# Channel attention: part of the softmax denominator through accumulating DMAs, a one-column border from PSUM, and chain openings on ScalarE

## The chip, the cores and the metric

The kernel runs as one program on one NeuronCore of a Trainium2 chip. The time is device microseconds from launch to end, the median of several executions. Engines are named as in the profile: PE is TensorE (matmuls and transposes), PEld its weight loads, DVE is VectorE, ACT is ScalarE, POOL is GpSimd, SP is SyncE.

## What is computed

Four residual layers on `x` of shape 4 x 256 x 64 x 64, each behind a group normalisation. The change lies in the third, the channel attention. Cut to what matters:

```python
half = cout // 2
x_pad = jnp.pad(x, ((0, 0), (0, 0), (PAD, PAD), (PAD, PAD)))      # PAD = 3, K = 7
q    = jnp.einsum('bchw,oc->bohw', x, w_q)
kmap = jnp.einsum('bchw,oc->bohw', x_pad, w_k)
vmap = jnp.einsum('bchw,oc->bohw', x_pad, w_v)
kwin, vwin = _unfold2d(kmap, K), _unfold2d(vmap, K)               # 7 x 7 windows
kwin = jnp.concatenate([kwin[:, :half] + rel_h, kwin[:, half:] + rel_w], axis=1)
attn = jax.nn.softmax(q[..., None] * kwin.reshape(b, cout, h, w, K * K), axis=-1)
out  = jnp.sum(attn * vwin.reshape(b, cout, h, w, K * K), axis=-1)
x    = x + out
```

Every channel and pixel has its own softmax over the 49 taps of its window.

## The kernel before, in words

**Tiling.** `channel_attention` handles 16 bands of 16 image rows (4 images x 4). A band has 256 channels, two halves of 128 partitions, and each half is cut into two tiles of 8 rows, 512 pixels. So a band is four tiles, t = 0 to 3, and the layer is 64 tiles. A tile has 49 taps; tap j is written (o, i) = divmod(j, 7), and I call the seven taps of one o a row of taps.

**One tap, four engines.** DVE (`multiply`, L1991) writes (key window + bias) x query into one of three PSUM banks `stage`. PE (`shift`, L1677) subtracts an upper bound `top` from it by a matmul with minus the identity. ACT (`exponential`, L1845) writes the exponential into `se`, a ring of four rows of taps. POOL (`weigh`, L1892) multiplies by the value window, four taps and then three of a row in one instruction, into `ev`. PE adds up both: `sum_exponential` adds the exponential of tap j-2 into the bank `pe_sum`, `sum_weighted` adds the product of tap j-12 into `pv_sum`. Both use `add_up` (L1684): four 128 x 128 transposing matmuls that accumulate in PSUM.

**What orders the work.** There is no scheduler: each engine's queue is written out in tap order and waits on semaphores. PE's step j is: `sum_weighted` of j-12, `shift` of j, `sum_exponential` of j-2. `multiply` of tap j waits for the exponential of tap j-3, which frees its bank, so DVE is at most three taps ahead. `exponential` waits, at the first tap of a group, until the slot's old values have been added up and weighed.

**Extra work in the steps.** While half H is worked on, the next half is prepared. PE projects keys, queries and values into `pj` (`project`, L1666, at the steps of `PROJ_AT`: K1, K2, Q1, Q2 when t is even, V1 and V2 when t is odd; each has two matmuls, which the trace shows as two instructions each). ACT copies them out. DVE builds `near`, the largest and the smallest key of each row or column of seven, in two levels: `near_step_of` first takes pairs into `pair` (L1938, from `pj` and the keys), then reduces (L1946). For the half whose windows run along columns of the image (H even, built in t = 2) a border of 3 columns at both sides of `pair` is first filled by a `tensor_scalar` from the zero columns of the keys (L1931, four times per band). Then 34 links (`extreme_step`, at the steps `EXT_AT`, in even tiles from step 34 on and in odd tiles) turn `near` into the bound `top`: four chains of 7 additions and maxima (or minima), whose opening link is a `tensor_scalar` (L1965) and whose others are L1967, then products and maxima (L1974, L1976). DVE also inverts the denominator of the tile before (`invert`, L1999, steps 3, 5, 7, 9; `take_e_sums`, L1833, copies it out of PSUM at step 1), divides (L2007, step 12) and adds the residual (step 23).

The few lines that set PE's order in a tap:

```python
if not late and (t * NTAP + j >= V_LAG or not first):
    sum_weighted(n, *before(t, j, V_LAG), first=first)
shift(n, t, j)
if t * NTAP + j >= E_LAG or not first:
    sum_exponential(n, *before(t, j, E_LAG), first=first)
```

## Time and profile before

| | us |
|---|---|
| median of 3 runs | 8098.6 |
| lowest, highest | 8085.5, 8104.4 |
| span of the profiled execution | 8087.0 |
| of it, channel attention's 64 tiles | from about 3310 to 7405 |

The profiled execution itself is one of those whose span is 8087.0 us from the first to the last instruction; what lies around the span is 11.6 us against the median. Over the span PE is busy 93%, DVE 72%, POOL 56%, ACT 45%. Within channel attention (3600 to 7100 us) PE is busy 96%, DVE 91%, POOL 80% and ACT 50%.

The rows are read like this. A busy time is a share of an engine's own time; instructions of PE and DVE overlap a little with their successors, so what one of them costs in a dense stretch is the distance from its start to the next one's start, which the timeline shows. A bracket behind a row is the engine's idle time just before it and what ended it.

### The profile page before, as it was taken

To read this page: it belongs to the slowest core of one execution; us is meant where nothing else is said; L and a number is where in the kernel's file an instruction comes from. 1 tells how busy PE (TensorE), PEld (TensorE's weight loads), DVE (VectorE), ACT (ScalarE), POOL (GpSimd) and SP (SyncE) were. 2 spreads that over 40 slices of the span, in tenths; PEclk is the share of its full clock that TensorE was granted. 3 is DMA by queue.
4 is the path that set the end of the run, shared out by engine and by line. 5 is a ranking of instruction groups with operands and counts; after the bars stand their busy time and mean duration, and the time that the engine had idled before them with its cause. 6 is when DMAs were issued, how large, how long until landed. Compare 5 with 4: busy or idle time off the path is not lost. (4 is left out here: it accounts for less than half of the span.)

```text
span 8087.0 us, 141762 instructions
## 1 busy us (share of the span) xinstructions
PE 7551.7 (93%) x55106; PEld 6507.3 (80%) x55106; DVE 5845.1 (72%) x8981; ACT 3601.8 (45%) x6912; POOL 4566.7 (56%) x2002
## 2 busy tenths in 40 slices
PE   5999998999997998799999999999999999997999
PEld 4777776789997775588888888888888888886899
DVE  5666665334442555798998999999999989996664
ACT  3556554333332332345445454545545454554222
POOL 3555552033331001588777887878878787886232
PEclk9999998999998999899999999999999999998999
DMA  3111114855557772100000000000000000002452
GB/s 144 57 60 66 56 62 137 277 152 146 148 146 215 220 206 85 25 19 19 24 21 21 18 18 26 18 20 19 20 27 18 15 21 24 23 12 79 144 163 81
DMA packets 633017, 617.20 MB, mean 76 GB/s; under 512 B 465525, under 2 KB 498421, under 8 KB 627174
## 3 DMA queue, kind: packets, MB, share of 16 engines
q1 hardware_dynamic: 581318, 483.44, 21.5%
q0 software_dynamic: 33856, 96.69, 3.3%
q10 hardware_dynamic: 17376, 30.54, 1.0%
q8 instruction: 330, 5.41, 0.3%
q14 instruction: 137, 1.12, 0.0%
HBM read 397.01 MB, written 193.76 MB: 73 GB/s over the span
## 5 line engine op out<-in xcount | busy, mean ns | idle before, releaser
L1892 POOL TENSOR_TENSOR e_ev<-e_se,e_v 128x2048 f32<-128x2048 f32 (+1 forms) x896 | 3307.9, 3712 | 858.9 <-ACT e_se L1845 856.5
L1845 ACT ACTIVATE e_se<-e_stage 128x512 f32<-128x512 f32 x3136 | 1868.5, 598 | 2038.3 <-PE e_stage L1677 1991.5
L1991 DVE SCALAR_TENSOR_TENSOR e_stage<-e_k,e_rl,e_qp 128x512 f32<-128x512 f32 x3136 | 2299.7, 746 | 250.1 <-ACT e_se L1845 199.3
L1684 PE MATMUL e_pe_sum<-e_ident,e_se 128*128 128x128 f32 x12544 | 1888.5, 273 | 16.4 <-ACT e_se L1845 12.2
L1684 PE MATMUL e_pv_sum<-e_ident,e_ev 128*128 128x128 f32 x12544 | 1881.1, 273 | 0.5 <-POOL e_ev L1892 0.5
L1684 PEld LDWEIGHTS e_pe_sum<-e_ident,e_se 128*128 128x128 f32 x12544 | 1556.7, 140 | 261.3 <-ACT e_es L1833 21.8
L1677 PE MATMUL e_stage<-e_top,e_minus 128*128 128x512 f32 x3136 | 1513.4, 483 | 163.1 <-DVE e_stage L1991 160.9
L1684 PEld LDWEIGHTS e_pv_sum<-e_ident,e_ev 128*128 128x128 f32 x12544 | 1483.0, 141 | 205.7 <-issue 203.7
L911 POOL DMA_DIRECT2D agg<-c_ot x384 | 334.6, 874 | 880.6 <-ACT c_ot L989 771.0
L403 POOL TENSOR_TENSOR a_pr<-a_pr,a_rden 128x480 f32<-128x480 f32 x512 | 494.6, 987 | 547.2 <-DVE a_rden L636 547.2
L1677 PEld LDWEIGHTS e_stage<-e_top,e_minus 128*128 128x128 f32 x3136 | 598.2, 191 | 219.6 <-DVE e_stage L1991 185.2
L596 ACT ACTIVATE a_pr<-a_ps,a_nmax 128x240 f32<-128x240 f32 x1024 | 459.2, 460 | 386.1 <-DVE a_nmax L630 386.1
L1967 DVE SCALAR_TENSOR_TENSOR e_ext<-e_near,e_rl,e_ext 128x512 f32<-128x512 f32 x768 | 574.9, 749 | 0.9
L948 PE MATMUL c_pa<-c_x_high,c_w_high 128*128 128x448 f32 (+1 forms) x1440 | 523.0, 363 | 33.2 <-DVE c_w_low L1014 33.2
L630 DVE TENSOR_REDUCE a_nmax<-a_ps 128x2 f32<-128x480 f32 x512 | 312.8, 652 | 292.4 <-PE a_ps L484 285.2
L948 PE MATMUL c_pa<-c_x_low,c_w_high 128*128 128x448 f32 (+1 forms) x1440 | 522.7, 363 | 0.0
L948 PE MATMUL c_pa<-c_x_high,c_w_low 128*128 128x448 f32 (+1 forms) x1440 | 522.5, 363 | 0.0
L2287 PE MATMUL f_pc<-f_x_high,f_w_high 128*128 128x256 f32 x1536 | 440.4, 287 | 14.0 <-DVE f_xr L2467 11.8
L1946 DVE TENSOR_REDUCE e_near<-e_pair 128x192 f32<-128x768 f32 (+1 forms) x392 | 436.1, 1113 | 0.5
L2287 PE MATMUL f_pc<-f_x_low,f_w_high 128*128 128x256 f32 x1536 | 434.8, 283 | 0.0
L2287 PE MATMUL f_pc<-f_x_high,f_w_low 128*128 128x256 f32 x1536 | 434.2, 283 | 0.0
L2244 POOL TENSOR_TENSOR f_x_low<-f_xt,f_x_high 128x2560 fp32r<-128x2560 f32 x32 | 186.2, 5819 | 438.3 <-ACT f_x_high L2321 406.6
(175 smaller groups left out, 11663.9 us busy)
## 6 DMA issues: line engine op xcount, KB each, us to landing
qkv<-b_ot SPq DMA_DIRECT2D x120, 512.0 KB, 5.9
c_xt<-qkv SPq DMA_DIRECT2D x384, 160.0 KB, 3.8
agg<-c_ot POOLq DMA_DIRECT2D x384, 160.0 KB, 2.5
f_ws<-in_L_w_sets SPq DMA_DIRECT2D x32, 1152.0 KB, 8.0
a_xb<-in_x SPq DMA_DIRECT2D x24, 768.0 KB, 5.1
a_xr<-in_x SPq DMA_DIRECT2D x32, 512.0 KB, 3.8
x<-a_xr SPq DMA_DIRECT2D x32, 512.0 KB, 2.7
b_xc<-x SPq DMA_DIRECT2D x32, 512.0 KB, 6.0
```

What stands on the lines that cost most here:

```text
L403: nc.gpsimd.tensor_tensor(w, w, by, ALU.mult).then_inc(normalised, 1)
L596: last = nc.scalar.activation(pr[P % BUF][:, i, e, :], ps[:, 2 * s + i, e * NK:(e + 1) * NK], ACT.Exp, bias=nmax[P % BUF][:, i, e:e + 1], ...
L911: pool.dma_start(dst, ot[u][:, b]).then_inc(stored[u], 16)
L948: last = nc.tensor.matmul(pa[:, u, r, 0:(last_ - first) * WW].rearrange("p (k c) -> p k c", c=WW), lhsT=w[u][:, dx].rearrange("p o y -> p ...
L1677: nc.tensor.matmul(stage[:, bank_of(t, j), :], lhsT=minus[:], rhs=top[h][:, u * TPX:(u + 1) * TPX], start=False, stop=True, skip_group_che ...
L1684: last = nc.tensor.matmul(acc[:, c * PART:(c + 1) * PART], lhsT=src[:, c * PART:(c + 1) * PART], rhs=ident[:], is_transpose=True, start=j ...
L1845: nc.scalar.activation(se[(t * K2 + o) % NSE][:, i], stage[:, bank_of(t, j), :], ACT.Exp)\
L1892: nc.gpsimd.tensor_tensor(split(ev[(t * NG2 + g) % NEV][:, 0:size]), split(se[(t * K2 + o) % NSE][:, i:i + size]), window(v[h], h, u, o, i ...
L1946: nc.vector.tensor_reduce(grid(near[:, i])[:, first + low:first + low + part, PAD:PAD + WW], pairs, AX.XY, op)\
L1967: nc.vector.scalar_tensor_tensor(rows(ext[:]), win, r[:, o:o + 1], rows(ext[:]), ALU.add, op)\
L1991: nc.vector.scalar_tensor_tensor(rows(stage[:, bank_of(t, j), :]), win, rl[:, h, o:o + 1], rows(qp[:]), ALU.add, ALU.mult).then_inc(multip ...
L2287: last = nc.tensor.matmul(pc[:, m, s], lhsT=w[:, m, s * KW3 + dy, h], rhs=x[u][:, s, h, rows], start=dy == 0 and h == 0 and i == 0, stop=d ...
```

## The change

Three edits, all in channel attention.

1. **Exponentials partly added by DMA.** The exponentials of the first four taps of row 0 go into a new buffer `acc` instead of `se` (two buffers, by tile parity). For rows 1 to 4 of taps (`GATHERED`), after POOL has weighed the row, POOL issues a DMA that adds the row's first four exponentials (128 x 2048 numbers, 1 MiB) onto `acc`. Each such DMA waits until the one before has landed. PE no longer adds these 20 taps one by one. It adds the four columns of `acc` at steps 44 to 47, and before the first it waits until all four DMAs of the tile have landed. So PE makes 33 sums of exponentials per tile instead of 49.
2. **Border.** The `tensor_scalar` over 3 columns at both sides becomes a `tensor_tensor` over one column at the left, from the zero column of the keys and the first projected column in PSUM; the wait behind it is dropped.
3. **Opening links.** The four opening links of the chains are made by ACT (an Identity activation with bias) instead of DVE; `EXT_AT` is spread anew, with three places instead of one between an opening link and the next.

```diff
+        acc = [sb(f"acc{u}", [PART, ROW_PARTS[0][1], TPX]) for u in range(2)]
...
+        GATHERED = (1, 2, 3, 4)
+        NACC = ROW_PARTS[0][1]
+        DIRECT = [j for j in range(NTAP) if j % K2 >= NACC or j // K2 not in (0, *GATHERED)]
+        NES = len(DIRECT) + NACC
+        ACC_AT = (44, 45, 46, 47)
...
-        EXT_AT = [EXT_FREE[s * len(EXT_FREE) // NEXT_] for s in range(NEXT_)]
+        OPENS = [0, CHAIN[0], 2 * CHAIN[0], 2 * CHAIN[0] + CHAIN[1]]
+        LINK_AT = [sum(3 if i - 1 in OPENS else 1 for i in range(1, s + 1)) for s in range(NEXT_ + 1)]
+        EXT_AT = [EXT_FREE[LINK_AT[s] * len(EXT_FREE) // LINK_AT[-1]] for s in range(NEXT_)]
...
+            def sum_gathered(n, t, i):
+
+                if i == 0:
+                    pe.wait_ge(gathered, gathers(n, t, K2))
+                add_up(pe_sum, acc[t % 2][:, i], False, False).then_inc(e_summed, 1)
...
-                if t * NTAP + j >= E_LAG or not first:
+                if (t * NTAP + j >= E_LAG or not first) and before(t, j, E_LAG)[1] in DIRECT:
                     sum_exponential(n, *before(t, j, E_LAG), first=first)
+                if j in ACC_AT:
+                    sum_gathered(n, t, ACC_AT.index(j))
...
+            def open_extreme(H, s):
+
+                act.wait_ge(near_step, nears(H + 1))
+                act.wait_ge(ext_step, exts(H, s))
...
+                nc.scalar.activation(rows(ext[:]), win, ACT.Identity, bias=rl[:, h, 0:1]).then_inc(ext_step, 1)
...
+            def gather(n, t, o):
+
+                if o == GATHERED[0]:
+                    pool.wait_ge(weighted, tiles(n, t, NG2, 1))
+                else:
+                    pool.wait_ge(gathered, gathers(n, t, o - 1))
+                flat = lambda x: x.rearrange("p i n -> p (i n)")
+                pool.dma_start(flat(acc[t % 2][:]), flat(se[(t * K2 + o) % NSE][:, 0:NACC]), accum_op=ALU.add).then_inc(gathered, 16)
...
                         weigh(n, t, g, first=n == 0)
+                        if g % 2 and g // 2 in GATHERED:
+                            gather(n, t, g // 2)
...
-                        edge = [[PW, size], [WW + 2, 2], [1, PAD]]
-                        nc.vector.tensor_scalar(bass.AP(tensor=a.tensor, offset=a.offset, ap=[a.ap[0]] + edge),
-                                                bass.AP(tensor=z.tensor, offset=z.offset, ap=[z.ap[0]] + edge), 0.0, None, op)\
-                            .then_inc(near_step, 1)
-                        dve.wait_ge(near_step, nears(H) + near_before(H, s) + 1)
+                        edge = lambda t: grid(t)[:, first:first + size, PAD - 1:PAD]
+                        nc.vector.tensor_tensor(edge(pair[:, i]), packed(pj, p)[:, :, 0:1], edge(k[0][:]), op).then_inc(near_step, 1)
```

`exponential` follows: it writes to `acc` or `se`, and before it reuses the first four columns of a gathered row's slot it waits for that row's DMA instead of PE's sums.

What stands on POOL in the first tile of channel attention, rows 0 to 2 of taps. Before:

```order
L1892 TENSOR_TENSOR e_ev0<-e_se0,e_v0 128x2048
L1892 TENSOR_TENSOR e_ev1<-e_se0,e_v0 128x1536
L1892 TENSOR_TENSOR e_ev2<-e_se1,e_v0 128x2048
L1892 TENSOR_TENSOR e_ev3<-e_se1,e_v0 128x1536
L1892 TENSOR_TENSOR e_ev0<-e_se2,e_v0 128x2048
L1892 TENSOR_TENSOR e_ev1<-e_se2,e_v0 128x1536
```

The change, at the same place:

```order
L1949 TENSOR_TENSOR e_ev0<-e_acc0,e_v0 128x2048
L1949 TENSOR_TENSOR e_ev1<-e_se0,e_v0 128x1536
L1949 TENSOR_TENSOR e_ev2<-e_se1,e_v0 128x2048
L1949 TENSOR_TENSOR e_ev3<-e_se1,e_v0 128x1536
L1960 DMA e_acc0<-e_se1 128x2048
L1949 TENSOR_TENSOR e_ev0<-e_se2,e_v0 128x2048
L1949 TENSOR_TENSOR e_ev1<-e_se2,e_v0 128x1536
L1960 DMA e_acc0<-e_se2 128x2048
```

A DMA stands behind each pair of weighing instructions of rows 1 to 4, and each of the last three waits for the one ahead of it.

What stands on PE at steps 44 and 45 of the first band's last tile (`e_stage` is the shift, `e_pe_sum` the sum of exponentials, `e_pv_sum` the sum of products). Before:

```order
L1677 MATMUL e_stage<-e_top1,e_minus 128x512
L1684 MATMUL e_pe_sum<-e_ident,e_se3 128x128 x4
L1684 MATMUL e_pv_sum<-e_ident,e_ev3 128x128 x4
L1677 MATMUL e_stage<-e_top1,e_minus 128x512
L1684 MATMUL e_pe_sum<-e_ident,e_se3 128x128 x4
L1684 MATMUL e_pv_sum<-e_ident,e_ev3 128x128 x4
```

The change, at the same place:

```order
L1703 MATMUL e_stage<-e_top1,e_minus 128x512
L1710 MATMUL e_pe_sum<-e_ident,e_se3 128x128 x4
L1710 MATMUL e_pe_sum<-e_ident,e_acc1 128x128 x4
L1710 MATMUL e_pv_sum<-e_ident,e_ev3 128x128 x4
L1703 MATMUL e_stage<-e_top1,e_minus 128x512
L1710 MATMUL e_pe_sum<-e_ident,e_se3 128x128 x4
L1710 MATMUL e_pe_sum<-e_ident,e_acc1 128x128 x4
L1710 MATMUL e_pv_sum<-e_ident,e_ev3 128x128 x4
```

Each of the steps 44 to 47 has four more transposes, and the first of them, behind the shift of tap 44, carries the wait for the DMAs.

What stands on DVE where the border is made, in t = 2 of the first band. Before:

```order
L1931 TENSOR_SCALAR e_pair<-e_k0 128x8x2x3
L1938 TENSOR_TENSOR e_pair<-e_pj,e_k0 128x8x64
L1991 SCALAR_TENSOR_TENSOR e_stage<-e_k1,e_rl,e_qp 128x512
L1931 TENSOR_SCALAR e_pair<-e_k0 128x8x2x3
L1938 TENSOR_TENSOR e_pair<-e_pj,e_k0 128x8x64
```

The change, at the same place:

```order
L1997 TENSOR_TENSOR e_pair<-e_pj,e_k0 128x8
L2001 TENSOR_TENSOR e_pair<-e_pj,e_k0 128x8x64
L2049 SCALAR_TENSOR_TENSOR e_stage<-e_k1,e_rl,e_qp 128x512
L1997 TENSOR_TENSOR e_pair<-e_pj,e_k0 128x8
L2001 TENSOR_TENSOR e_pair<-e_pj,e_k0 128x8x64
```

The same places in the queue hold an instruction on 8 elements per partition instead of 48, with one operand in PSUM.

## Rows read from the trace of the kernel before

**Rows 1.** Page, part 1: busy time (share of the span) x instructions.

```profile
PE 7551.7 (93%) x55106; PEld 6507.3 (80%) x55106; DVE 5845.1 (72%) x8981; ACT 3601.8 (45%) x6912; POOL 4566.7 (56%) x2002
```

**Rows 2.** One line's instructions (L1833, once per tile): ns min/median/max, first and last start.

```profile
L1833 ACT ACTIVATE e_es<-e_pe_sum x64: 589/592/597, 3374.9 to 7408.1; 128x512 f32<-128x512 f32 x64
```

**Rows 3.** Busy us (instructions) of PE, PEld, DVE, ACT, POOL; clock; DMA: one band's tiles.

```profile
4849.35:4916.82 67.47, 64.48 (x464) 54.20 (x462) 63.47 (x85) 32.18 (x56) 51.48 (x15) 1.00 0.09 29
4916.82:4976.51 59.69, 58.80 (x456) 52.47 (x454) 52.99 (x78) 33.73 (x56) 51.14 (x15) 1.00 0.15 32
4976.51:5046.23 69.72, 64.38 (x464) 55.35 (x462) 63.43 (x88) 32.17 (x57) 52.20 (x15) 0.98 0.07 22
5046.23:5105.11 58.88, 58.80 (x456) 52.51 (x454) 53.20 (x78) 31.10 (x55) 51.96 (x15) 1.00 0.01 1
```

**Rows 4.** Timeline of PE in t = 2: start us, us, instruction.

```profile
5015.64 1.04 PE L1666 MATMUL e_pj<-e_xb,e_wt 128*128 128x512 f32 x2
5016.53 0.60 PE L1684 MATMUL e_pv_sum<-e_ident,e_ev 128*128 128x128 f32 x4
5016.88 0.48 PE L1677 MATMUL e_stage<-e_top,e_minus 128*128 128x512 f32 x1
5017.19 0.60 PE L1684 MATMUL e_pe_sum<-e_ident,e_se 128*128 128x128 f32 x4
5017.63 0.60 PE L1684 MATMUL e_pv_sum<-e_ident,e_ev 128*128 128x128 f32 x4
5017.99 0.48 PE L1677 MATMUL e_stage<-e_top,e_minus 128*128 128x512 f32 x1
```

**Rows 5.** Timeline of DVE in t = 3.

```profile
5048.30 0.74 DVE L1967 SCALAR_TENSOR_TENSOR e_ext<-e_near,e_rl,e_ext 128x512 f32<-128x512 f32 x1
5048.95 0.75 DVE L1991 SCALAR_TENSOR_TENSOR e_stage<-e_k,e_rl,e_qp 128x512 f32<-128x512 f32 x1
5049.61 0.94 DVE L1999 RECIPROCAL e_rs<-e_es 128x128 f32<-128x128 f32 x1
5050.47 0.67 DVE L1991 SCALAR_TENSOR_TENSOR e_stage<-e_k,e_rl,e_qp 128x512 f32<-128x512 f32 x1
```

**Rows 6.** Timeline of POOL in t = 3: each row is one row of taps.

```profile
5091.77 7.41 POOL L1892 TENSOR_TENSOR e_ev<-e_se,e_v 128x2048 f32<-128x2048 f32 x2 [0.34 <-ACT e_se L1845]
5099.52 7.37 POOL L1892 TENSOR_TENSOR e_ev<-e_se,e_v 128x2048 f32<-128x2048 f32 x2 [0.34 <-ACT e_se L1845]
```

**Rows 7.** Groups by line and form, DVE, 3600 to 7100 us: busy, mean ns.

```profile
L1946 DVE TENSOR_REDUCE e_near<-e_pair 128x192 f32<-128x768 f32 x224 | 273.1, 1219 | 0.0
...
L1931 DVE TENSOR_SCALAR e_pair<-e_k 128x48 f32<-128x48 f32 x56 | 81.2, 1450 | 25.2 <-ACT e_k L1819 25.2
```

**Rows 8.** Line L1931: ns min/median/max, first and last start.

```profile
L1931 DVE TENSOR_SCALAR e_pair<-e_k x72: 167/193/3391, 3259.9 to 7064.9; 128x48 f32<-128x48 f32 x64, 128x18 f32<-128x18 f32 x8
```

**Rows 9.** Timeline of DVE at a border instruction of t = 2.

```profile
5001.56 3.38 DVE L1931 TENSOR_SCALAR e_pair<-e_k 128x48 f32<-128x48 f32 x1
```

**Rows 10.** Timeline of POOL at the same place.

```profile
5000.72 4.18 POOL L1892 TENSOR_TENSOR e_ev<-e_se,e_v 128x2048 f32<-128x2048 f32 x1 [4.64 <-ACT e_se L1845]
```

**Rows 11.** Timeline of PE at the same place.

```profile
5006.39 0.80 PE L1677 MATMUL e_stage<-e_top,e_minus 128*128 128x512 f32 x1 [3.30 <-DVE e_stage L1991]
```

**Rows 12.** Busy times just behind it; columns as in rows 3.

```profile
5006.40:5009.80 3.40, 3.40 (x14) 3.20 (x15) 3.40 (x5) 0.60 (x1) 1.91 (x1) 0.50 0.00 0
```

**Rows 13.** DMA issues of the whole execution: queue, count, KB each, median us to landing.

```profile
agg<-c_ot POOLq DMA_DIRECT2D x384, 160.0 KB, 2.5
...
x<-e_xr SPq DMA_DIRECT2D x32, 512.0 KB, 2.7
...
e_k<-e_k ACTq DMA_DIRECT2D x24, 210.0 KB, 2.2
```

**Rows 14.** DMA issues, 3600 to 7100 us.

```profile
stats<-e_st SPq DMA_DIRECT2D x28, 6.0 KB, 1.4
```

**Rows 15.** Groups by line and form, POOL, whole execution.

```profile
L911 POOL DMA_DIRECT2D agg<-c_ot x384 | 334.6, 874 | 880.6 <-ACT c_ot L989 771.0 <-issue 109.6
```

## What I predict, before the run

> **What bounds the kernel now.** I read the page first [rows 1]: PE is busy 93% of the span, but its share counts overlapped ends, so it names a suspect and no more. The change lies in channel attention, whose 64 tiles are told apart by the copy of the denominator: 63 distances in 7408.1 - 3374.9 = 4033.2 us, 64.0 us a tile [rows 2]. The table by tile [rows 3] then shows two kinds. Tiles t = 1 and 3 take 59.7 and 58.9 us, with PE at 58.8 and DVE at 53; tiles t = 0 and 2 take 67.5 and 69.7, with PE at 64.4 and DVE at 63.4. POOL has some 52 us of work in each, and where it is idle it waits for exponentials [rows 6]. No engine alone explains the even tiles, so I priced each step.
>
> From start to start, a tap costs PE 5017.99 - 5016.88 = 1.11 us: shift 0.31, sum of exponentials 0.44, sum of products 0.36 [rows 4]. A projection's pair of matmul records costs 0.89. DVE pays 0.66 for a `multiply` or a link, 0.86 for an inversion [rows 5], and 1.22 in the mean for a reduction to `near` [rows 7], where those along columns (t = 0) take more and those of t = 2 less. POOL pays 7.4 for a row of taps, and starts rows 7.75 apart where nothing else happens [rows 6], which is 7 x 1.107: there the row is PE's. Since DVE may be only three taps ahead, a row of taps takes the larger of its PE work and its DVE work. Summed over seven rows this gives 58.2 us for t = 1 and for t = 3, where PE is the larger nearly everywhere: 49 x 1.107 + 4 x 0.88 for V1 and V2 + 0.43 for turning the output back. For t = 0 the rows are 7.8, 9.5, 12.5, 11.2, 9.5, 7.8, 7.8 = 66.0 (rows 2 and 3 are DVE's, with the reductions in them), for t = 2 they are 7.8, 9.5, 10.3, 9.5, 9.5, 7.8, 7.8 = 62.1. Against rows 3, t = 0, 1 and 3 are explained within 1.5 us; t = 2 is 7.6 short.
>
> That gap is the border. Its 48-element instruction has a mean of 1450 ns [rows 7] but a median of 193 [rows 8]: a few wait. One takes 3.38 us and ends at 5004.94 [rows 9], just as POOL's instruction beside it ends at 5004.90 [rows 10]. PE then sits idle for 3.30 us [rows 11], and the granted clock falls to 0.50, its lower level of 1.2 GHz, for 3.4 us [rows 12], in which PE does half its work.
>
> **Edit 2, the border.** Four instructions per band lose 1.25 us each: 5.0 us. The halved stretch goes too: 3.4 / 2 = 1.7 us. The new instruction has 8 elements instead of 48 and takes an operand from PSUM, like the taps, which run on beside POOL's work [rows 5, 6]; I give it 0.1. If it were held up as the old one was, the 5.0 and the 1.7 would stay. Sum -6.7 us per band, all of it on the path, since DVE was late there.
>
> **Edit 3, opening links.** DVE loses 8 x 0.66 = 5.3 us per band, ACT gains 8 x 0.6 at 32 us of work in a tile of 60 to 70 [rows 3]. It counts only in rows that DVE sets; it is in the sums of the next part. ACT's waits there are for links that DVE made at an earlier step, so nothing new queues behind them, except at step 47 of even tiles, where the last exponential comes 0.5 us later (covered by two exponentials in hand; without them 0.5 x 32 = 16 us in all).
>
> **Edit 1, what PE gains.** Rows 0 to 4 lose four sums each, 4 x 0.43 = 1.7 us, row 6 gains 1.7: PE's tile falls by 6.8. But DVE is next. With the same rule, row by row, and edit 3 in it: t = 1 and 3 become 7.6, 8.9, 6.5, 7.8, 6.4 (all DVE), 7.9, 9.5 (PE) = 54.6, so -3.6 each. t = 0 becomes 6.3, 8.1, 12.5, 11.2, 8.4, 7.8, 9.5 = 63.8 (-2.2), because rows 2 and 3 were DVE's already, and t = 2 becomes 6.3, 8.4, 10.1, 9.3, 7.8, 7.8, 9.5 = 59.1 (-3.0). Sum -12.4 per band. With edit 2: -19.1. The rule averages over a row, but the spared taps are four in a row beside three full ones; for that I take back 2, as 0.5 a tile. So **-17.1 per band** before any new wait. POOL allows it: 7 x 7.45 + 4 x 0.8 for issues, near its own stores' 0.87 us [rows 15], is 55.3 per tile.
>
> **Edit 1, the new wait.** Behind the shift of tap 44 PE waits for the tile's fourth DMA, and with PE everything stops within three taps: shifts, so ACT, DVE's banks, and soon POOL. When does it land? Let d be the time from issue to landing. In t = 1 and 3, POOL needs 7.4 + 0.85 + 0.1 = 8.3 us a row in rows 1 to 4 while the others would feed it one in 6.4 to 7.8. From the exponential of tap 10, POOL takes 4 x 7.45 + 3 x 0.85 = 32.4 us to the end of row 4, the exponential of tap 34 comes after 3.8 + 6.5 + 7.8 + 6.4 = 24.5, so POOL ends 7.9 us behind tap 34. PE reaches the wait 10 steps of 1.107 later less the 0.8 between a shift and its exponential's end: 10.3. The stall is 7.9 + 0.1 + d - 10.3 = **d - 2.3**. In even tiles POOL keeps up, ends 4.0 us behind tap 34, and the stall is d - 6.2 (t = 2: d - 5.9).
>
> No row shows an accumulating DMA, so d is bounded. Plain transfers: 6 KB take 1.4 us [rows 14] and 512 KB 2.7 [rows 13], so 1 MiB of data costs 2.6; the 210 KB copy from SBUF to SBUF takes 2.2 [rows 13], of which 0.5 is data, so 1.7 is fixed; POOL's own 160 KB store takes 2.5, so its fixed part is 2.1. The lower end is a plain copy, 1.7 + 2.6 = 4.3. Adding means that source and target are both read: 1.7 + 5.2 = 6.9. The upper end is three passes one after another on POOL's slower fixed part of 2.1: 2.1 + 7.8 = 9.9. I take 6.9, since only the second read is sure. The issue may cost nothing beyond its cover in even tiles, and up to 1 us more each if it grows with size.
>
> The Trainium skill bears on this: its page Collectives: The Full Stack (Part 3) says that a reduction by DMA runs at half the rate of a copy because of the second source read, about 31 GB/s per DMA engine halved. By that and the 2.0 us fixed cost of DMA: Bandwidth & Descriptors (Anatomy of one DMA), an estimate for d is 6.2 instead of 6.9, and the stalls would be 0.7 shorter in each tile, which makes the sum 45 us better. No run so far shows it.
>
> With d = 6.9: stalls of 4.6 in t = 1 and 3, 0.7 in t = 0, 1.0 in t = 2. Stalls of that length cost clock as well: 3.30 idle was followed by the halved stretch [rows 11, 12], worth 1.7; PE is the bound behind the wait. I take 1.2 for each odd tile, as not every such gap need do it. Sum 2 x 5.8 + 1.7 = **+13.3 per band**.
>
> **Sum.** -17.1 + 13.3 = -3.8 per band, x 16 = -61 us. On the span of 8087.0 this is 8026; the median of the runs lies 11.6 above the span, so 8037.
>
> **Rivals.**
> A. The DMA is as fast as a plain copy, d = 4.3. Stalls 2.0 in odd tiles, none in even ones, no clock loss: -17.1 + 4.0 = -13.1, x 16 = -210: 7889. For it: the DMA engines are nearly idle here [rows 3]. Against it: the sum needs the old value.
> B. Slower: **the DMAs queue up on POOL.** Each of the last three waits for the one before, issued 8.3 us earlier in odd tiles. From d = 8.3 on, POOL itself stalls in front of the next row, and the stall at tap 44 comes on top. At d = 9.2: odd tiles 6.9 + 1.7 clock + 3 x 0.9 = 11.3, even ones 3.0 and 3.3, and 1.7 clock in one of them: +30.6 - 17.1 = +13.5, x 16 = +216: 8315. At 9.9 it is some 330. For it: three passes are within the bounds. It turns slower than before already at d = 7.8, where stalls and clock eat the 17.1.
> C. The stall just eats the gain, d about 7.5 to 7.8: 8085 to 8110.
> D. The relief of PE does nothing because DVE or POOL bounds every tile, and only the border counts: -6.7 x 16 = -107 less the stalls, which lands between my forecast and C. It is in my range.
>
> **Chances.** Forecast with D: 0.42. A: 0.18. B: 0.30. C: 0.10. A time within 0.2% (16 us) of the present one is what a measurement of this kernel can't tell from no change. Of the forecast's 0.42 some 0.04 lies within that and 0.01 above it, of C 0.05 within and 0.04 above, so: faster 0.56, same 0.09, slower 0.35. The range must hold A and most of B: 7880 to 8310.
>
> **What would show it.** After the run: sums of exponentials 33 x 4 x 64 = 8448 transposes, not 12544; the border instruction near 0.1 us with no idle PE behind it; about 4.6 us of PE idle per odd tile in front of the sum from `acc`, released by the DMA, and under 1 us in even ones; issue to landing near 6.9; odd tiles near 61, t = 0 near 67, t = 2 near 63.5. The forecast is wrong if d lies outside 5.5 to 7.5, if POOL's issues take over 1.5 us, if POOL waits for a DMA, or if the rows of taps don't follow the larger of PE and DVE.

## The result, and the profile after

The change takes 8169.9 us (8157.3 to 8178.3, four runs) against 8096.7 for the kernel before on the same chip: a ratio of 1.0089, interval 1.0074 to 1.0104. It is 73 us slower, where I had forecast 60 faster. The profiled execution has a span of 8176.6 us, 89.6 above that of before. The time given for a kernel is the median of its runs; one run, of the kernel with three rows by DMA, took 14692.6 us and stands in no median.

Page, busy times and granted clock (the answers to [rows 1]), then the copy of the denominator once per tile (to [rows 2]):

```profile
PE 7321.9 (90%) x51010; PEld 6136.8 (75%) x51010; DVE 5647.0 (69%) x8853; ACT 3648.5 (45%) x7040; POOL 4774.8 (58%) x2258
...
PEclk9999998999998998899999999999999999998999
```

```profile
L1866 ACT ACTIVATE e_es<-e_pe_sum x64: 587/592/597, 3396.1 to 7496.3; 128x512 f32<-128x512 f32 x64
```

PE's busy time is 230 us lower than before, so the change does what it says, and the time is longer all the same. The 63 distances between tiles add up to 7496.3 - 3396.1 = 4100.2 us, before 4033.2: 67 of the 89.6 us lie there. (What starts ahead of the first tile moves by some 20 us between kernels that are the same up to there, so I read the kernels below by these 63 distances and by their medians, and nothing from the stretch ahead.)

One band's four tiles, as in [rows 3] (busy us of PE, PEld, DVE, ACT, POOL; granted clock; DMA share, GB/s):

```profile
4891.02:4959.74 68.72, 59.35 (x400) 47.43 (x398) 61.38 (x81) 32.89 (x59) 54.89 (x19) 1.00 0.39 90
4959.74:5022.57 62.83, 56.41 (x392) 47.44 (x390) 52.16 (x77) 34.59 (x59) 55.06 (x19) 0.97 0.46 97
5022.57:5086.41 63.84, 58.16 (x400) 47.28 (x398) 55.88 (x85) 32.69 (x59) 54.79 (x19) 1.00 0.40 90
5086.41:5147.62 61.21, 54.72 (x392) 45.93 (x390) 51.71 (x77) 31.89 (x57) 55.02 (x19) 1.00 0.34 70
```

In the odd tiles (second and fourth line) PE's busy time fell by 2.4 and 4.1 us, and the tiles are 3.1 and 2.3 us longer. No engine is busy for more than 92% of any of the four. The new wait stands on PE. Timeline of PE at tap 44 of the fourth of these tiles, then of the tile behind it (start, us; in brackets the idle time ahead and what ended it):

```profile
5138.90 0.66 PE L1710 MATMUL e_pe_sum<-e_ident,e_acc 128*128 128x128 f32 x4 [3.25 <-DMA e_acc<-e_se]
```

```profile
5205.53 0.60 PE L1710 MATMUL e_pe_sum<-e_ident,e_se 128*128 128x128 f32 x4
5208.33 0.87 PE L1710 MATMUL e_pe_sum<-e_ident,e_acc 128*128 128x128 f32 x4 [2.21 <-DMA e_acc<-e_se]
5209.00 1.06 PE L1710 MATMUL e_pv_sum<-e_ident,e_ev 128*128 128x128 f32 x4
5209.71 0.77 PE L1703 MATMUL e_stage<-e_top,e_minus 128*128 128x512 f32 x1
5210.28 1.06 PE L1710 MATMUL e_pe_sum<-e_ident,e_se 128*128 128x128 f32 x4
```

Behind the second wait the same instructions take 1.06 us instead of 0.60: the granted clock is at its lower level, 0.50 or 1.2 GHz, for 3.41 us (busy times and clock of the stretch):

```profile
5208.64:5212.05 3.41, 3.41 (x18) 3.23 (x16) 0.76 (x1) 0.60 (x1) 1.07 (x2) 0.50 0.00 0
```

Waits over 3600 to 7100 us (who, for whom: us in total, times, longest), and the DMAs there (issue: count, ns min/median/max):

```profile
DVE e_stage L2049 <- ACT e_se L1888: 348.3, 358, 8.8
PE e_stage L1703 <- DVE e_stage L2049: 261.1, 473, 2.6
...
PE e_pe_sum L1710 <- DMA e_acc<-e_se: 115.7, 53, 4.6
...
POOL e_acc L1960 <- DMA e_acc<-e_se: 10.2, 12, 1.4
```

```profile
L1960 POOL DMA_DIRECT2D e_acc<-e_se x216: 813/872/1527, 3602.6 to 7095.1; - x108
...
DMA to landing us min/median/max: 6.9/7.4/10.7
```

PE waits for the DMAs in nearly every tile (53 times in some 54 tiles), 2.2 us each. POOL rarely waits for one (12 times). The two remaining witnesses that I had named, the border instruction and the transposes from `acc` (the page has 7424 from `se`, 8448 in all):

```profile
L1997 DVE TENSOR_TENSOR e_pair<-e_pj,e_k x72: 154/168/173, 3267.7 to 7133.7; 128x8 f32<-128x8 f32 x64, 128x3 f32<-128x3 f32 x8
```

```profile
L1710 PE MATMUL e_pe_sum<-e_ident,e_acc 128*128 128x128 f32 x1024 | 175.1, 298 | 143.9 <-DMA e_acc<-e_se 143.9
```

So the wait is there at about the size that I had forecast for the band, and the forecast was still 133 us off. Which of the terms failed, the trace of the whole change can't say. The experiments take them one at a time.

### The profile page after: what moved, and what is told of

Same layout as the page of the kernel before. It is cut to its first block and busy times, and to the rows that moved or that the text cites. A ratio compares the mean times of both kernels' runs of the same rounds, so it can differ in the third digit from the quotient of the medians.

```text
span 8176.6 us, 133952 instructions
## 1 busy us (share of the span) xinstructions
PE 7321.9 (90%) x51010; PEld 6136.8 (75%) x51010; DVE 5647.0 (69%) x8853; ACT 3648.5 (45%) x7040; POOL 4774.8 (58%) x2258
## 5 line engine op out<-in xcount | busy, mean ns | idle before, releaser
L1949 POOL TENSOR_TENSOR e_ev<-e_se,e_v 128x1536 f32<-128x1536 f32 (+1 forms) x832 | 3092.8, 3797 | 574.0 <-ACT e_se L1888 537.2
L1888 ACT ACTIVATE e_se<-e_stage 128x512 f32<-128x512 f32 x2880 | 1700.2, 598 | 1971.2 <-PE e_stage L1703 1952.0
L1710 PE MATMUL e_pv_sum<-e_ident,e_ev 128*128 128x128 f32 x12544 | 1903.5, 275 | 10.4 <-POOL e_ev L1949 4.4
L1703 PE MATMUL e_stage<-e_top,e_minus 128*128 128x512 f32 x3136 | 1542.9, 492 | 342.2 <-DVE e_stage L2049 333.1
L1710 PEld LDWEIGHTS e_pv_sum<-e_ident,e_ev 128*128 128x128 f32 x12544 | 1528.7, 142 | 309.7 <-issue 200.9
L1710 PE MATMUL e_pe_sum<-e_ident,e_se 128*128 128x128 f32 x7424 | 1136.1, 276 | 0.0
L1710 PEld LDWEIGHTS e_pe_sum<-e_ident,e_se 128*128 128x128 f32 x7424 | 941.9, 142 | 139.5 <-issue 11.2
L2025 DVE SCALAR_TENSOR_TENSOR e_ext<-e_near,e_rl,e_ext 128x512 f32<-128x512 f32 x768 | 575.4, 749 | 12.0 <-ACT e_ext L1897 11.2
L2345 PE MATMUL f_pc<-f_x_high,f_w_high 128*128 128x256 f32 x1536 | 441.7, 288 | 12.5 <-DVE f_xr L2525 10.3
```

The source lines that it names most:

```text
L1703: nc.tensor.matmul(stage[:, bank_of(t, j), :], lhsT=minus[:], rhs=top[h][:, u * TPX:(u + 1) * TPX], start=False, stop=True, skip_group_che ...
L1710: last = nc.tensor.matmul(total[:, c * PART:(c + 1) * PART], lhsT=src[:, c * PART:(c + 1) * PART], rhs=ident[:], is_transpose=True, start= ...
L1888: nc.scalar.activation(exps(t, j), stage[:, bank_of(t, j), :], ACT.Exp).then_inc(exp_done, 1)
L1949: nc.gpsimd.tensor_tensor(split(ev[(t * NG2 + g) % NEV][:, 0:size]), split(exps(t, o * K2 + i, size)), window(v[h], h, u, o, i, size), ALU ...
L2025: nc.vector.scalar_tensor_tensor(rows(ext[:]), win, r[:, o:o + 1], rows(ext[:]), ALU.add, op)\
L2345: last = nc.tensor.matmul(pc[:, m, s], lhsT=w[:, m, s * KW3 + dy, h], rhs=x[u][:, s, h, rows], start=dy == 0 and h == 0 and i == 0, stop=d ...
```

## The experiments

The kernel before took 8092 to 8095 us beside all of them.

### Edit 2 alone

The kernel before with the new border instruction and nothing else (the second hunk of the diff from `edge =` on).

> The kernel before with edit 2 alone (the one-column border). Theory from the prediction: 1.25 us of each of four border instructions and one halved stretch per band go, 6.7 us per band, 16 bands: about 107 us faster than before, 7990. The idle time of PE of 3.3 us in t = 2 is gone and at most two or three halved stretches are left. Rival: behind the border the same rows of taps are held by PE's projections anyway, and under 50 us show.

It takes 7989.1 us, ratio 0.9870 (0.9854 to 0.9887): -105 us.

```profile
L1833 ACT ACTIVATE e_es<-e_pe_sum x64: 587/591/597, 3376.7 to 7302.9; 128x512 f32<-128x512 f32 x64
```

The distances fall by 4033.2 - 3926.2 = 107.0, all of it in t = 2 (63.2 us in the mean instead of 70.3; the others move by 0.2 at most). Stretches at the lower clock between the first and the last copy of the denominator fall from 16 to 1. The border theory stands, size and place: -6.7 x 16 = -107 was the forecast. The edit changes the instruction's size, its kind, one operand's place and the wait behind it at once; which of these frees it no run tells apart.

### Edits 2 and 3

The same, with the openings on ACT and the new `EXT_AT`.

> The kernel before with edits 2 and 3 (border and opening links), without the DMAs. Theory: opening links count only in rows of taps that DVE sets, and PE sets nearly all while it makes all 49 sums, so edit 3 adds 0 to -15 us to edit 2: about 7985. Rival: DVE is the bound at the level of single taps, and edit 3 gives its full 5.3 us per band, 85 us: about 7905. Second rival: the link that ACT makes comes late for DVE, and it costs some 20 us.

7994.1 us, ratio 0.9876 (0.9860 to 0.9893), distances 3927.2. Taking 5.3 us per band off DVE is worth nothing while PE makes all its sums: no row of taps moves by more than 0.1 us. DVE's idle time only moves. Over 3600 to 7100 us it waits 237 us for exponentials instead of the 149 with edit 2 alone, and for the query copy behind the opening at step 47 56 times instead of 28, 40.6 us instead of 22.3:

```profile
L1828 ACT ACTIVATE e_qp<-e_q x56: 596/600/604, 3630.6 to 7068.3; 128x512 f32<-128x512 f32 x56
...
who waited for it (us, times):
  DVE e_stage L1998: 40.6, 56
```

The cover that I had named for that step, two exponentials in hand, isn't there in full; but it costs 1.3 us of DVE's time per band, which PE doesn't see.

### The whole change without its new wait, and without its DMAs

Two kernels. In the first POOL issues all DMAs, and PE adds four columns of a constant instead of `acc`, without waiting. ACT, which in the change waits for PE's sums before it reuses `acc`, here waits for the DMAs of the tile before last.

```diff
-                if i == 0:
-                    pe.wait_ge(gathered, gathers(n, t, K2))
-                add_up(pe_sum, acc[t % 2][:, i], False, False).then_inc(e_summed, 1)
+                add_up(pe_sum, wt[:, 0].rearrange("p h o -> p (h o)"), False, False).then_inc(e_summed, 1)
```

> The changed kernel, whose DMAs still run and are waited for on POOL and ACT, but PE doesn't wait for them: the four sums at steps 44 to 47 read a constant buffer instead of acc, so the gathered exponentials are left out of the denominator. Theory of the wait: the stall at tap 44 (1.8, 2.0, 1.8 and 3.3 us in the four tiles of a band) and the halved clock behind it (some 28 more stretches of 3.4 us than before, half of each lost) are 8.8 + 3 to 5 us per band, so this is 190 to 220 us faster than the change: about 7960, and the halved stretches fall to under 10. Rival, contention: the DMAs themselves slow POOL's weighing (4.2 to 4.5 us) and the issues, and without the wait at least half of the loss stays: above 8060.

In the second the DMAs are gone too, with ACT's waits for them; PE's four sums read `acc` again, which holds row 0 alone, and the gathered exponentials of rows 1 to 4 are in no sum.

```diff
-                if i == 0:
-                    pe.wait_ge(gathered, gathers(n, t, K2))
                 add_up(pe_sum, acc[t % 2][:, i], False, False).then_inc(e_summed, 1)
...
-                        if g % 2 and g // 2 in GATHERED:
-                            gather(n, t, g // 2)
```

> As no_wait, and the DMAs are not issued at all: PE sums acc, which holds row 0 only; the exponentials of rows 1 to 4, columns 0 to 3, are left out of the denominator. Theory of the wait: POOL has room for the four issues, so this is within 30 us of no_wait. Rival, contention: it is over 60 us faster than no_wait, POOL's weighing is back at 4.2 us everywhere. It also prices the relief of PE and DVE by itself: the prediction had 19.1 - 2 = 17.1 us per band, 274 us below before, 7823; if taps don't average over a row, it is less, about 7900.

Without the wait: 7966.9 us, ratio 0.9845 (0.9828 to 0.9861). The wait costs 8169.9 - 7966.9 = **203 us**, 12.7 per band; I had 13.3. Of the 43 stretches at the lower clock 14 are left, where I had expected under 10; before there were 16. Without the DMAs too: 7956.2 us, ratio 0.9831 (0.9815 to 0.9848). The transfers and their issues by themselves cost **11 us**.

What is left when both are gone is PE's relief in its pure form, and it is small: 7956.2 against 7994.1 for edits 2 and 3 is **-38 us**, 2.4 per band, where I had 12.4 - 2 = 10.4. Neither time that I had named for this kernel came, not the 7823 of the sum nor the 7900 without averaging. From the kernel before to the change, step by step, this is -105 (border) + 5 (openings) - 38 (relief) + 11 (DMAs) + 203 (wait) = +76. Each number is the difference of two neighbours in one chain of kernels, so the sum has to come out near the measured +73 and proves nothing; what it shows is the size of each. One term is wrong by 128 us, the others by 11 at most.

Here is the band of that last kernel, columns as before:

```profile
4803.42:4870.42 67.00, 59.15 (x400) 47.46 (x398) 61.39 (x81) 32.87 (x58) 51.63 (x15) 1.00 0.08 30
4870.42:4931.75 61.33, 56.18 (x392) 47.34 (x390) 52.15 (x77) 34.58 (x59) 51.64 (x15) 0.97 0.14 30
4931.75:4993.90 62.15, 57.95 (x400) 47.30 (x398) 55.88 (x85) 32.68 (x59) 51.60 (x15) 1.00 0.07 25
4993.90:5051.64 57.74, 54.50 (x392) 45.94 (x390) 51.73 (x77) 31.90 (x57) 51.59 (x15) 1.00 0.00 1
```

The first tile takes 67.0 us with no engine above 61.4. My rule, the larger of PE's and DVE's work in each row of taps, gave 63.8 for it. The times of the rows of taps, from the starts of the exponentials and as means over 14 bands, show where it broke:

| row of taps | 0 | 1 | 2 | 3 | 4 | 5 | 6 |
|---|---|---|---|---|---|---|---|
| t = 0, by the rule | 6.3 | 8.1 | 12.5 | 11.2 | 8.4 | 7.8 | 9.5 |
| t = 0, edits 2 and 3 | 8.9 | 9.9 | 12.3 | 11.2 | 10.5 | 7.8 | 7.7 |
| t = 0, relief alone | 8.5 | 9.9 | 12.4 | 11.1 | 8.9 | 7.8 | 9.5 |
| t = 3, by the rule | 7.6 | 8.9 | 6.5 | 7.8 | 6.4 | 7.9 | 9.5 |
| t = 3, edits 2 and 3 | 9.2 | 10.4 | 8.2 | 7.8 | 7.8 | 7.8 | 7.9 |
| t = 3, relief alone | 9.1 | 9.8 | 6.8 | 7.6 | 6.9 | 8.0 | 9.5 |

Rows 2 to 6 are within 0.6 us of the rule, but for row 4 of t = 1, in which ACT normalises the next band (9.2 instead of 6.4; it took 8.8 with edits 2 and 3, so the 1.4 us forecast there did not come either). Rows 0 and 1 are 0.9 to 2.2 us above it in all four tiles (11.8 per band), and they gain 0.6 us at most. Over a whole tile the relief was to be 2.2, 3.6, 3.0 and 3.6 us for t = 0 to 3; it is 0.3, -0.4, 0.8 and 1.3. The reason stands in the timeline of PE in row 1 of t = 0 (taps 7 to 13; after the whole change, where these rows take the same time):

```profile
4899.20 1.04 PE L1692 MATMUL e_pj<-e_xb,e_wt 128*128 128x512 f32 x2
4900.08 0.60 PE L1710 MATMUL e_pv_sum<-e_ident,e_ev 128*128 128x128 f32 x4
4900.43 0.48 PE L1703 MATMUL e_stage<-e_top,e_minus 128*128 128x512 f32 x1
4900.76 0.60 PE L1710 MATMUL e_pv_sum<-e_ident,e_ev 128*128 128x128 f32 x4
4901.11 0.48 PE L1703 MATMUL e_stage<-e_top,e_minus 128*128 128x512 f32 x1
4901.42 0.60 PE L1710 MATMUL e_pv_sum<-e_ident,e_ev 128*128 128x128 f32 x4
4901.78 0.48 PE L1703 MATMUL e_stage<-e_top,e_minus 128*128 128x512 f32 x1
4903.69 0.50 PE L1703 MATMUL e_stage<-e_top,e_minus 128*128 128x512 f32 x1 [1.43 <-DVE e_stage L2049]
```

and of DVE beside it:

```profile
4898.80 1.55 DVE L2049 SCALAR_TENSOR_TENSOR e_stage<-e_k,e_rl,e_qp 128x512 f32<-128x512 f32 x2
4902.28 0.69 DVE L2001 TENSOR_TENSOR e_pair<-e_pj,e_k 128x512 f32<-128x512 f32 x1 [1.93 <-ACT e_k L1852]
4902.88 0.74 DVE L2049 SCALAR_TENSOR_TENSOR e_stage<-e_k,e_rl,e_qp 128x512 f32<-128x512 f32 x1
```

Two matmuls of the projection sit on each of two steps that still make all their sums: such a step takes PE 1.99 us. Then come steps without a sum of exponentials, and PE takes 0.68 each (4900.43 to 4901.11 to 4901.78). It eats up its three taps in hand in 2 us, while DVE waits for the projected keys, and then it waits 1.43 us for DVE. The spared sums shorten the very steps on which PE was not late. A stock of three taps can't carry the gain from one end of a row to the other. That is the reading of row 1. Row 0 of the even tiles, 2.2 and 1.4 us above the rule, has DVE's inversions in it, the first of which waits for the copied denominator; what makes it longer no run told apart.

### Plain copies in place of the adding ones

`accum_op` is left out: each DMA overwrites `acc` instead of adding to it. All waits stay.

> The changed kernel with plain copies in place of accumulating DMAs (acc then holds row 4's exponentials only, so rows 0 to 3 of the first four columns are left out). It prices the second read: if that is what makes 7.4 us to landing out of my lower end of 4.3, landing falls to 4.3 to 5, the stalls of even tiles go and those of odd tiles fall to about 0.5, and the time comes near that without the wait: 7970 to 8000. Rival: the fixed part is larger than I took and the data term smaller; landing stays above 6 and the time above 8080.

7973.2 us in a single run. Issue and landing:

```profile
L1960 POOL DMA_DIRECT2D e_acc<-e_se x225: 592/594/603, 3611.0 to 7098.3; - x113
...
DMA to landing us min/median/max: 4.4/4.7/8.1
```

```profile
PE e_pe_sum L1710 <- DMA e_acc<-e_se: 1.5, 3, 0.7
```

Adding makes a 1 MiB DMA land in 7.4 us instead of 4.7, and its issue take 0.87 instead of 0.59. Less a fixed part of 2.1, which is my estimate from POOL's own stores [rows 13], the data take 2.6 and 5.3 us: twice. By the Trainium skill (Collectives: The Full Stack, Part 3) a reduction by DMA has twice the traffic on the reading side and so half the rate; with that fixed part this pair of runs agrees. My 6.9 had the same doubling on a fixed part of 1.7; the page's rate on its 2.0 gave 6.2, which is too short. With the shorter landing the wait is gone (1.5 us in all), and the time of this one run is 7973 where rival A had 7889: the relief that A counted on is mostly not there.

### Zeros added before the wait

Three sums of a zero buffer stand in front of the wait, 3 x 0.44 us of work per tile that changes nothing.

```diff
                 if i == 0:
+                    for _ in range(3):
+                        add_up(pe_sum, nil[:], False, False)
                     pe.wait_ge(gathered, gathers(n, t, K2))
```

> The changed kernel with three more sums at step 44 of each tile, ahead of the wait for the DMAs, that add a buffer of zeros to the denominator: 3 x 0.44 = 1.3 us of work where PE would sit idle. The wait stays. In the trace of the change every gap before the sum from acc of up to 1.8 us is followed by no halved stretch, and nearly every one of 2.08 us and more by one. Theory of the clock: the gaps of 2.1 to 3.5 us fall to 0.8 to 2.2, most of the some 28 extra halved stretches go, each worth 1.7 us, so this is 30 to 50 us FASTER than the change although PE does more: about 8130. Rival: the halved stretches cost nothing, since PE isn't the bound there; then it is the same as the change, or up to 20 us slower where gaps are shorter than the filling: 8170 to 8190.

8155.3 us, ratio 1.0077 (1.0060 to 1.0093) against the change's 1.0089: PE has 84 us more work, and the kernel is no slower. By the medians it is 15 us faster, by the distances 11 (4088.8 against 4100.2), and against the kernel before, run beside each, also 11 (62.5 and 73.2 above it). The wait shrinks, its end comes only 0.1 to 0.3 us later, counted from tap 34's exponential, and the time at the lower clock between the first and the last copy of the denominator falls from 167 to 102 us (43 and 28 stretches).

```profile
PE e_pe_sum L1711 <- DMA e_acc<-e_se: 64.0, 49, 3.7
```

That speaks for a price of the clock that can be taken away without touching the DMA, but the intervals overlap, so it isn't shown. The price would be smaller than I had it: 11 to 15 us for 15 stretches is 0.7 to 1.0 us each, not 1.7, and the 30 to 50 us that I had expected are out.

### The sums of `acc` later

They move from steps 44 to 47 to the last two steps.

```diff
-        ACC_AT = (44, 45, 46, 47)
+        ACC_AT = (47, 47, 48, 48)
...
-                if j in ACC_AT:
-                    sum_gathered(n, t, ACC_AT.index(j))
+                for i, a in enumerate(ACC_AT):
+                    if a == j:
+                        sum_gathered(n, t, i)
```

> The changed kernel with the four sums from acc, and the wait ahead of them, at steps 47 and 48 (two each) instead of 44 to 47. The same work on PE, the wait 3.3 us later. Theory of the wait: medians of 1.5 to 2.8 us of idle at tap 44 go to zero, the halved stretches with them, and all but the longest waits vanish: 7970 to 7985, near the kernel without the wait, some 190 us below the change, and a little below the border alone (7989). Rival: POOL or ACT is late by then anyway (the slot's reuse, the denominator's copy at step 1 comes sooner behind the sums), and the wait only moves: above 8050.

7970.7 us, ratio 0.9848 (0.9832 to 0.9864), 199 us below the change:

```profile
PE e_pe_sum L1710 <- DMA e_acc<-e_se: 3.1, 3, 1.1
```

Three steps of 1.1 us cover nearly every wait (2.2 in the mean, 4.6 at most). The wait and not the DMA was what cost the change its 200 us, and it is a matter of three steps.

### Three rows by DMA instead of four

`GATHERED = (1, 2, 3)`; the sums stay at steps 44 to 47. The last DMA is issued a row of taps earlier, and PE makes four more sums per tile.

> The changed kernel with DMAs for rows 1 to 3 of taps only; row 4 is summed tap by tap, steps 44 to 47 keep their four sums from acc. The last DMA is issued a row earlier. Theory: no stall at tap 44 in any tile; row 4 takes the time that it takes without the relief (10.5, 8.8, 9.5, 7.8 us against 8.9, 9.2, 8.2, 6.9 in the kernel without DMAs), 3.3 us per band or 53 us above the kernel without the wait: about 8015, which is 25 us slower than the border alone. Rival: POOL still lags in odd tiles and the wait stays: above 8060.

8024.7 us, ratio 0.9919 (0.9899 to 0.9939), within 10 us of what I expected; no gap on PE in front of a sum from `acc` is longer than 0.3 us. Row 4 takes 10.6, 9.1, 9.9 and 8.1 us again (8.9, 9.2, 8.2, 6.9 with four rows), 4.5 us per band and so more than the 54 us that it loses to the late sum: row 4 is one of those in which the relief does come out (10.5 to 8.9 us for t = 0 in the table above).

### Projections moved onto spared steps

If the reason given above is right, the relief comes out when the projections move to steps 2 to 5 of a row, counted from 0, where the sums of exponentials are spared. This is the late sum with

```diff
-        PROJ_AT = ({0: "K0", 7: "K1", 14: "K2", 24: "Q1", 29: "Q2"}, {2: "V0", 6: "V1", 12: "V2"})
+        PROJ_AT = ({0: "K0", 9: "K1", 16: "K2", 25: "Q1", 30: "Q2"}, {2: "V0", 9: "V1", 16: "V2"})
...
-        DIVIDE_AT, BACK_AT, ADD_AT = 12, 20, 23
-        STATS_AT = (25, 27)
+        DIVIDE_AT, BACK_AT, ADD_AT = 12, 22, 25
+        STATS_AT = (27, 29)
```

and all steps of `NEAR` two later.

> As late_sum, and PE's projections of K1, K2, V1, V2 and Q1, Q2 are moved from steps 7, 14, 6, 12, 24, 29 to 9, 16, 9, 16, 25, 30, with the reductions of near, the turning back and the residual two steps later. Theory: the relief of PE by 16 sums brought only 38 us in the kernel without DMAs because it lies in steps 2 to 5 of a row of seven, while the projections lie in steps 0, 1 and 6, which still make all sums (1.99 us a step); moved onto spared steps they fit in 1.55. I expect rows 1 and 2 of even tiles and rows 0, 1 and 2 of odd tiles to lose 0.5 to 1.5 us each, 3 to 5 us per band: 50 to 80 us below late_sum, about 7910. Rival: DVE's own work sets those rows, and the shift brings under 15 us, or the later reductions push DVE past the links and cost.

7989.7 us, ratio 0.9882 (0.9864 to 0.9901): no gain. By tile it is one gain and one loss. t = 0, 2 and 3 fall from 67.9, 62.4, 58.1 to 67.3, 61.1, 57.3; row 1 takes 8.6 to 8.9 us instead of 9.8 to 10.0 in all of them. But t = 1 rises from 60.5 to 65.3, all of it in row 4, 14.5 us instead of 9.4. ACT's normalisation of the next band, at step 30, waits for the last part of that band's load, the coefficients. The load is issued when V2 has been projected, and V2 I had moved from step 12 to 16:

```profile
ACT e_xb L1800 <- DMA e_cf<-coef: 55.6, 14, 4.8
```

Counted from the first exponential of t = 1, the load is issued at 21.7 us instead of 18.1 and the coefficients land at 39.7 instead of 31.8 (27.6 in the kernel before, where no adding DMAs run beside it); the exponential ahead of the normalisation ends at 34.5. ACT waits 4.0 us in each of 14 bands, with the exponentials queued behind it. So the same once more, with the normalisation six steps later:

```diff
-        NORM_AT = 30
+        NORM_AT = 36
```

> As aligned, and ACT normalises the next band's input at step 36 of t = 1 instead of 30. In aligned the two steps gained in rows 0 to 2 were given back at one place: tap 30 of t = 1 took 7.4 us (3.4 in the change), because the load of that input starts only when V2 is projected (now step 16, before 12) and ACT waited 55.6 us in 14 bands for the last part of it. Theory: t = 1 falls from 65.3 to 59 to 59.5 us, the rest stays, 6 us per band: 7895 to 7905, and the alignment is worth 65 to 75 us against late_sum. Rival: the wait only moves to step 36, or the input is then late for the next half's keys: above 7950.

**7913.8 us**, ratio 0.9784 (0.9768 to 0.9801): 57 us below the late sum, 256 below the change and 2.2% below the kernel before.

```profile
L1865 ACT ACTIVATE e_es<-e_pe_sum x64: 587/592/597, 3376.0 to 7223.7; 128x512 f32<-128x512 f32 x64
```

DVE's waits for the projected keys over 3600 to 7100 us (us in total, times), in the late sum and then here:

```profile
its engine sat idle before it (us, times) until:
  ACT e_k L1853: 48.6, 26
```

```profile
  ACT e_k L1851: 6.2, 22
```

PE's busy time over the span is that of the late sum within 13 us (7242.1 and 7254.8): the work is the same, only its place has changed, row 1 has gained 0.9 to 1.2 us in each tile, and DVE hardly waits for keys any more. That bears the reason out for row 1. It isn't the whole of it: 57 us came back of the 128 that were missing, below the 65 to 75 that I had expected. Row 0 of the odd tiles gained 0.9 and their row 2 lost 1.0, row 0 of the even ones did not move, and what holds them stays open. Of the 3.9 us per band t = 1 gains 1.2; how much of that is the later normalisation, and how much of the rest DVE's reductions two steps later, I did not run apart.

### The openings back on DVE

Edit 3 undone, first in the late sum, then in the version just shown.

> late_sum without edit 3: the opening links back on DVE, at the old places. Beside PE's 49 sums edit 3 was worth nothing (7994 against 7989). Theory: with PE relieved DVE sets most rows 0 to 4, and in those 5.3 us of links per band weigh: 30 to 60 us slower than late_sum, 8000 to 8030. Rival: the opening links lie at steps 34, 47, 16 and 32 of which PE sets most, and it is within 15 us of late_sum.

7952.9 us, ratio 0.9831 (0.9814 to 0.9847), against 7970.7 with edit 3. I had expected DVE's 5.3 us per band to come back as 30 to 60 us; it went the other way. By the distances it is 10 us (3896.0 against 3906.4); the rest lies ahead of the first tile, where runs differ by as much. The waits for the query copy fall from 56 to 28 again, and t = 1 and 3 gain 0.8 and 0.5 us, of which t = 0 and 2 give 0.6 back.

> The version with the late sum, the projections moved to steps of a row whose sums are spared and the normalisation at step 36, with the opening links given back to DVE (edit 3 undone). Theory: with PE relieved, edit 3 costs as much here as it did with the projections in their old places, where undoing it took the late sum from 7970.7 to 7952.9 us (18 us). Then this one gives 7913.8 - 18 = about 7896 us. Rival: with the projections on spared steps the rows 0 to 2 are bound by DVE, so that there DVE's eight openings (8 x 0.66 = 5.3 us per band) come back onto the path: at half of that, +2.7 x 16 = 42 us against the 18 gained, 7938 us. Within 5 us of 7914 neither is borne out.

7934.5 us, ratio 0.9807 (0.9793 to 0.9821), against 7913.8: here edit 3 is worth 21 us by the medians and 27 by the distances (3874.3 against 3847.6), though the intervals of the ratios overlap a little. The rival's size came, but not its place. Rows 0 to 2, which it named, hold 0.4 of the 1.7 us per band; 1.0 lies in t = 1, above all in rows 4 (7.6 instead of 6.9) and 6 (11.2 instead of 10.5). The same edit costs 10 us in the tiles of one arrangement and brings 27 in those of another; why its sign turns in t = 1 stays open.

## Why the prediction was wrong, point by point

- **The border** (-6.7 per band): right in mechanism, size and place; -105 us measured against -107.
- **The opening links**: I gave them no term of their own, and alone they have none (7989.1 and 7994.1). The cover for the copy at step 47 was thinner than I said; the 16 us that I named as the price without it stand as 18 us of DVE's waiting, none of them on PE's path there.
- **PE's relief**: this is the step that failed. "A row of taps takes the larger of its PE work and its DVE work" gave -12.4 per band, and I took back 2 for averaging within a row. Measured: -2.4 per band (7956.2 against 7994.1). The rule misses by 1 to 2 us in rows 0 and 1. In row 1 the projections stand mostly on steps that still make all sums (0, 1 and 6 of a row), and DVE waits for the projected keys; moving them gave 57 of the 128 us back. Why row 0 is late, and row 4 of t = 1 does not fall, is shown by no run. In rows 0 and 1 of t = 0 the rule was already 1.2 and 0.4 us too low before the change; I had compared whole tiles, where this went under in the 1.5 us that I allowed. The correction needed was 10, not 2. It makes 128 of the 133 us by which the forecast was off.
- **The landing time** d: 7.4 in the median instead of 6.9, with the second read as the cause, as I took it. It is longer, 9.9 in the mean, for the first DMA of t = 1, where a band's loads run beside it; the fourth of a tile, which PE waits for, lands in 7.2 to 7.9.
- **The stalls**: 8.8 us of idle per band against 10.9 forecast, but 1.8, 2.0, 1.8 and 3.3 for t = 0 to 3 instead of 0.7, 4.6, 1.0 and 4.6. The odd tiles were to stall more because PE would outrun POOL in rows 0 to 4; PE gained less, so the exponentials came later and POOL ended row 4 only 5.9 and 6.6 us behind tap 34's instead of 7.9. In the even tiles POOL ends it 5.4 us behind instead of 4.0 and the fourth DMA lands in 7.2 us instead of 6.9, while PE comes 0.6 us later than I had it; why POOL is later there stays open, its weighing takes 4.2 and 3.2 us as before.
- **The clock and the restart**: 12.7 - 8.8 = 3.9 us per band beyond the idle time, where I had 2.4. Part of it is the lower clock; how it divides between clock and refilling the three banks stays open.
- **The sum**: -105 - 38 + 203 + 16 for the small ones. Wait and clock together were right within 10 us (213 against 203), which is why the forecast's error lies in the gain and not in the danger I had looked at longest.
- **The rivals**: A's stall vanishes with a plain landing as it said, but the time isn't 7889. B, DMAs queued on POOL, hardly happens (10.2 us of waiting in 12 cases). The outcome, +73 us, lies on B's side of zero, and nearest to it stands D with the stalls at full price. D said "-107 less the stalls", and -105 + 5 - 38 + 11 + 203 is what came; D's reason, that DVE or POOL bounds every tile, isn't what the rows of taps show: row 2 of the odd tiles and row 4 of t = 0, 2 and 3 did gain. I had put D into the forecast's chance and called it a point between the forecast and C; worked out with its own numbers, -107 + 213, it is +106, slower than before. That sum stood on the page and wasn't made.

## What to carry to other kernels

When one engine is relieved in some steps and not in others, compare step by step which engine is late at each, over a distance no longer than the buffers between them (here three taps); an average over more than that shows a gain that can't be had. Put heavy side work on the steps that were relieved, and then look at which transfer is released at its old place and who waits for that. A result that comes by DMA should be consumed as late as the tile allows: three steps were worth 199 us here.

## What I had not expected of the hardware

- **Short gaps and the clock.** Of the change's 64 tiles I set the gap on PE in front of the wait's end beside the clock records: all 32 gaps of 1.8 us or less had no stretch at the lower clock near them, and 29 of the 32 of 2.08 us or more had one (the exceptions were 2.77, 2.81 and the 3.25 shown above). I had one row to go by, a gap of 3.3 us, and counted no clock for the shorter stalls of the even tiles.
- **The adding DMA slows POOL's own work.** In rows 3 to 5 of the odd tiles and row 5 of the even ones, where POOL starts its next instruction right behind the issue, the four-tap weighing takes 4.5 to 5.0 us in the mean and the three-tap one 3.4 to 3.9, instead of 4.2 and 3.2. With plain copies, issued at the same places, it stays at 4.2 and 3.2, and without DMAs as well. Timeline of POOL in the last tile shown above, rows 2 to 4 of taps (x2 is one row):

```profile
5107.69 7.34 POOL L1949 TENSOR_TENSOR e_ev<-e_se,e_v 128x2048 f32<-128x2048 f32 x2 [1.15 <-PE e_pv_sum L1710]
5114.97 0.88 POOL L1960 DMA_DIRECT2D e_acc<-e_se  x1
5115.57 7.68 POOL L1949 TENSOR_TENSOR e_ev<-e_se,e_v 128x2048 f32<-128x2048 f32 x2
5122.95 1.14 POOL L1960 DMA_DIRECT2D e_acc<-e_se  x1
5123.55 7.92 POOL L1949 TENSOR_TENSOR e_ev<-e_se,e_v 128x2048 f32<-128x2048 f32 x2
5130.90 1.41 POOL L1960 DMA_DIRECT2D e_acc<-e_se  x1
```

  The next instruction starts 0.60 us behind the issue's start, whatever the issue's record says, and the records of both grow from row to row. By the Trainium skill (SBUF — State Buffer, SBUF: two separate sides) a DMA can't be slowed by a compute operation nor the other way round; an apparent slowdown it puts down to DMAs issued from GpSimd, whose descriptors can't be written while VectorE holds the port that the two share. These rows differ from the first statement, and the second is another case, as here POOL's own compute is slowed. What slows it no run told apart.
- **Other transfers suffer too.** Over 3600 to 7100 us the 512 KB store `x<-e_xr` lands in 6.3 us instead of 2.7, the 210 KB copy of the values in 4.7 instead of 2.2, and the 2 KB of coefficients behind a band's load in 10.6 instead of 5.9. In the change nothing waited for them; with the projections moved, ACT waited for the last.
